# Delta attention: three groups of TensorE's queue moved behind the last key tile, two squares moved in ScalarE's

## The reference

```
q = silu(conv4(x @ Wq));  k, v = silu(conv4(x @ Wk)), silu(conv4(x @ Wv))      # 3 keys and values a token
for t:                                     # each head and batch
    S = S * exp(g_t)
    for i in range(3):
        S = S + beta_i * outer(k_i, v_i - k_i @ S)
    o_t = q_t @ S
out = (o * rsqrt(mean(o*o) + 1e-5) * rms_weight * silu(x @ Wg)) @ Wo
```

## Time and profile before

| | |
|---|---|
| time, median of 3 runs | 3211.24 us (3210.70 to 3217.59) |
| profiled execution, span | 3211.1 us |
| mean granted TensorE clock | 0.960 |
| TensorE matmul (PE) busy | 3002.0 us, 93% |
| TensorE weight load (PEld) busy | 2361.5 us, 74% |
| VectorE (DVE) busy | 2536.5 us, 79% |
| ScalarE (ACT) busy | 2251.8 us, 70% |
| GpSimd (POOL) busy | 1974.9 us, 62% |

### The profile page before, as it was taken

How to read it: one execution, slowest core, us unless ns; L and a number is a source line. 1 busy time by engine, 2 the same in 40 slices (tenths; PEclk the granted TensorE clock), 3 DMA queues, 4 the chain that set the end, 5 groups by cost and what they waited for, 6 DMA issues and landing times. The chain is left out here.

```text
span 3211.1 us, 83441 instructions
## 1 busy us (share of the span) xinstructions
PE 3002.0 (93%) x27212; PEld 2361.5 (74%) x27212; DVE 2536.5 (79%) x5859; ACT 2251.8 (70%) x6953; POOL 1974.9 (62%) x3125
## 2 busy tenths in 40 slices
PE   5569999999999999999999999999997999767999
PEld 3458888888888888888888888888876444455444
DVE  5669999999999999999999999999754454594554
ACT  4768888888888888888888888888643343412443
POOL 1588888888888888888888888888831000100000
PEclk8879999999999999999999999999998899957999
DMA  5457776767677766767777767677532332002322
GB/s 108 120 153 174 188 186 169 181 173 179 172 188 180 174 177 180 175 174 182 184 182 173 179 175 177 175 183 178 151 93 73 149 134 114 10 3 77 149 113 112
DMA packets 588205, 482.87 MB, mean 150 GB/s; under 512 B 464785, under 2 KB 504369, under 8 KB 581633
## 3 DMA queue, kind: packets, MB, share of 16 engines
q1 hardware_dynamic: 579328, 474.39, 55.8%
q10 hardware_dynamic: 8448, 3.15, 0.4%
HBM read 285.53 MB, written 191.86 MB: 149 GB/s over the span
## 5 line engine op out<-in xcount | busy, mean ns | idle before, releaser
L931 DVE SCALAR_TENSOR_TENSOR conv_k<-PP,tk,conv_k 128x256 f32<-128x256 f32 x1536 | 722.7, 479 | 61.8 <-ACT conv_k L766 33.6
L704 POOL TENSOR_TENSOR X<-X,tmp 96x31 f32<-96x31 f32 (+15 forms) x992 | 535.5, 540 | 77.7
L931 DVE SCALAR_TENSOR_TENSOR conv_v<-PP,tv,conv_v 128x256 f32<-128x256 f32 x1152 | 538.9, 477 | 44.9 <-ACT conv_v L766 35.3
L701 POOL TENSOR_TENSOR tmp<-At,X 96x31 f32<-96x31 f32 (+15 forms) x992 | 487.9, 492 | 63.1 <-DMA At<-n_d 4.9
L1100 PE MATMUL PP<-xn,wk 128*128 128x268 f32 x1024 | 341.9, 418 | 42.1 <-DVE conv_k L931 31.1
L687 POOL TENSOR_TENSOR rk<-ss,half 96x8 f32<-96x8 f32 x128 | 209.3, 1635 | 172.5 <-DVE ss L899 172.5
L669 POOL TENSOR_TENSOR Sg<-S,gend 128x512 f32<-128x512 f32 x256 | 266.8, 1042 | 60.4 <-DVE S L890 60.4
L738 ACT ACTIVATE recA<-TG,es 96x128 f32<-96x128 f32 x1024 | 285.4, 369 | 6.0 <-DVE es L924 6.0
L766 ACT ACTIVATE conv_k<-PP,tk 128x256 f32<-128x256 f32 x512 | 245.7, 482 | 58.7 <-PE PP L1100 51.9
L730 ACT ACTIVATE recA<-TG 128x128 f32<-128x128 f32 x1024 | 266.3, 273 | 24.2 <-PE TG L1151 24.2
L1064 PE MATMUL RB<-rhs,Yf 96*96 96x128 f32 x2048 | 269.0, 274 | 14.4 <-DVE rhs L879 14.4
(11 more groups left out here) (289 smaller groups left out, 6764.7 us busy)
## 6 DMA issues: line engine op xcount, KB each, us to landing
kqg_d<-kqgA SPq DMA_DIRECT2D x128, 512.0 KB, 6.1
kqgB<-kqg_d SPq DMA_DIRECT2D x128, 512.0 KB, 4.4
rec_d<-recA SPq DMA_DIRECT2D x128, 480.0 KB, 3.3
recB<-rec_d SPq DMA_DIRECT2D x128, 480.0 KB, 5.8
f1gates<-f1gates_d SPq DMA_DIRECT2D x24, 1024.0 KB, 6.6
f2gates<-f2gates_d SPq DMA_DIRECT2D x24, 1024.0 KB, 6.8
gdec<-gdec_d SPq DMA_DIRECT2D x128, 128.0 KB, 5.5
apk_d<-apkA SPq DMA_DIRECT2D x128, 128.0 KB, 3.3
```

The costliest lines, as they stand in the source:

```text
L701: nc.gpsimd.tensor_tensor(t, At[q % 2][:, j, j + 1:].unsqueeze(2).broadcast_to(sh), X[q % 2][:, j, 0:cols].unsqueeze(1).broadcast_to(sh), ...
L704: nc.gpsimd.tensor_tensor(x, x, t, ALU.subtract).then_inc(sub_ev, 1)
L931: return nc.vector.scalar_tensor_tensor(acc, src[:, :, j:j + SPAN], w[:, j:j + 1], acc, ALU.mult, ALU.add)
```

## The change

On TensorE, `wm(c)` and `o_(r, 0)` move behind `k_tile(f, 3)`, so that `wm`, both `o_` and `m3` follow one another. `o_(r, 1)` no longer waits for the square of half 0. On ScalarE both squares wait for the outputs of half 1 and stand behind `ksilu`; `w12` moves behind the first tap of the q tile, and `ksilu` ahead of the squares and `yev`. The scratch tile of the squares gets a part for each half.

```diff
-        osq = sb("osq", [128, 128])
+        osq = sb("osq", [128, NCC, 128])
...
-                need(act, o_mm[cc], N)
+                need(act, o_mm[1], N)
                 need(act, fs_ev, N - 1)
-                nc.scalar.activation(osq[:, :], o_ps[:, cc, :], ACT.Square, accum_out=mo[:, cc:cc + 1]).then_inc(mo_ev[cc], 1)
+                nc.scalar.activation(osq[:, cc, :], o_ps[:, cc, :], ACT.Square, accum_out=mo[:, cc:cc + 1]).then_inc(mo_ev[cc], 1)
...
                 tap0(f, "k1")
-                mo_(r, 0)
                 tap0(f, "k0")
                 kr(f - 1, 0)
                 vsilu(c)
                 kr(f - 1, 1)
                 tap0(f, "k2")
-                w12(c)
                 wev(r, 1)
                 q2_(f - 1)
                 tap0(f, "q")
+                w12(c)
+                ksilu(f)
+                mo_(r, 0)
                 mo_(r, 1)
                 yev(c)
-                ksilu(f)
                 qsilu(f)
...
                 need(pe, wev_ev[cc], N)
-                if cc:
-                    need(pe, mo_ev[0], N)
-                else:
+                if not cc:
                     need(pe, acc_ev, N - 1)
...
                 sr(r, 0)
                 k_tile(f, 1)
-                o_(r, 0)
                 k_tile(f, 0)
-                wm(c)
                 ks(r, 1)
                 gram(f - 1, 0)
                 k_tile(f, 2)
                 w_(r, 1)
                 gram(f - 1, 1)
                 k_tile(f, 3)
+                wm(c)
+                o_(r, 0)
                 o_(r, 1)
                 m3(c)
                 vtr(c, 1)
```

## The result

The changed kernel takes 3299.86 us (3298.34 to 3300.49, 4 runs) where the kernel before takes 3210.97 in the same session: a ratio of 1.0269, 95% interval 1.0254 to 1.0284. It is slower by 89 us; 96 were forecast. (The title counts three groups of TensorE's queue; two change their place, the merge and the output products of half 0.)

What follows compares the result with a forecast made beforehand. TensorE was taken to set the pass, with VectorE about 1.2 us to spare; 87 x 0.89 + 29 x 0.64 = 96 us, added to the median 3211.24, gave 3307 us, 8 in 10 range 3262 to 3350.

Steps and rivals of the forecast that it cites:

- TensorE's order would be stopped by k tile 0's bank: k tile 0 waits 0.33 us for VectorE's third tap of v tile 2, starting 7.98 us into the pass.
- 2.31 us from k tile 0 to `gram` 0: `gram` 0 waits for ScalarE's `kr` 0, behind the first tap of k tile 0; start at 10.29, wait 0.76 us.
- The arm over the three taps ends at the same time: VectorE's taps on k tile 0 lead to `rhs` 1, ready at 11.60, as `w_` 1 is reached at 11.70.
- The full pass 0.89 longer: `w_` 1 comes 0.65 us earlier, 1.54 of moved work follows; the full pass goes from 17.52 to 18.41 us.
- TensorE busy for about 1.2 us less: Sign expected in the profile after: TensorE's busy time about 1.2 us below a full pass of 18.2 to 18.5.
- The fourth pass 0.64 longer: In every fourth pass the 2 us copy starts 0.3 us earlier, giving back at most 0.25: 0.64 instead of 0.89.
- The edges: The last 11 passes, without a key part: taken at nothing, between -6 and +10 us in all.
- `m3` waits for nothing: ScalarE's `w12` runs within both groups of output products (0.92 us) ahead of `m3`; costed at nothing, up to 0.5 if late.
- The rival of the drains: Waits are covered and TensorE's saved drains, 0.50 us a pass, are all: 58 us faster, 3153 us; chance 0.08.
- The rival of the clock: TensorE's granted clock falls in one full pass in four after the new waits: 44 us more, 3351 us; chance 0.17.

Runs made afterwards that it cites:

- e4: The changed kernel with VectorE's `acc_` moved from ahead of the taps of v tile 2 to behind the third tap of k tile 1; 3291.89 us.
- e6: The changed kernel with ScalarE's `kr` of half 0 ahead of the first tap of k tile 0; 3437.07 us, ratio 1.0696.
- e3: The changed kernel with the output products of half 0 back ahead of k tile 0, so only the merge is moved; 3308.66 us, ratio 1.0289.
- e2: The changed kernel with the merge back behind k tile 0, so only the output products of half 0 are moved; 3246.66 us, ratio 1.0101.
- e5: The changed kernel with the merge and `w12` at their places of before and `acc_` behind the third tap of k tile 1; 3196.97 us, ratio 0.9947.
- e8: e5 with the 2 us copy of every fourth pass cut in two, the second part ahead of `wev(r, 0)`; 3173.05 us, ratio 0.9871.
- e9: e4 with GpSimd's solve cut to one column per product and difference; 3259.38 us, ratio 1.0143 to the kernel before.

## Why the prediction was right, step by step

**TensorE's order would be stopped by k tile 0's bank.** Right: 7.98 forecast, 7.97 measured, released by VectorE's conv_v. e4, which ends those taps earlier, moves k tile 0. `ks` 1 started at 8.57, 8.58 forecast.

**2.31 us from k tile 0 to `gram` 0.** Right: 10.29 forecast, 10.28 measured. The pass without a recurrence, in which this wait stands alone, gave the number. Its being a chain of two operands is what I missed: `es` had 0.19 us to spare by my count, 0.09 in the trace after, and none once the tap came earlier (e4). My 8.93 was its end in one pass, the earliest of three kinds: in the pass ahead of it, from 1200.01, it ended at 9.12. In the changed kernel it ends at 8.93, 9.02 and 9.11, and the last just binds: in the pass from 1240.98 `kr` 0 starts 0.42 behind its tap and not 0.38, and the pass takes 18.43. That is 0.05 us in one pass of four, 1.5 us in all; that it was not more was luck.

**The arm over the three taps ends at the same time.** Nearly: `rhs` 1 ended at 11.45 (11.54 forecast) and `w_` 1 started at 11.69 (11.70), so this arm had 0.18 to spare and not 0.10. Only e6 shows that it matters; forecast 3434, measured 3437.

**The full pass 0.89 longer.** 0.86 measured (18.41 and 18.38): the work behind the waits is as long as I summed it. One sign I gave was wrong: TensorE busy for about 1.2 us less. The windows show 18.38 - 17.62 = 0.76, since the profile's idle time begins at a modelled end; from start to start the waits are the 1.30 above (1.24 forecast).

**The fourth pass 0.64 longer.** Wrong in size, 0.31. I let the earlier copy give back at most the 0.25 us that TensorE waited there. But k tile 0 starts in that pass when VectorE's taps end, and these come earlier by the whole shift of the copy. In the changed kernel `At` starts at 1203.82, 0.20 ahead of its pass, and before at 1235.21, 0.16 into it, and the taps of v tile 2 end at 8.12 instead of 8.49. And k tile 0 stood 0.60 behind those taps in the fourth pass of before, against 0.42 in the full one. So it moves by 0.91, from 9.09 to 8.18 (0.60 ahead of `ks` 1, as in the full pass), where it moves by 0.37 in the full pass. This makes 29 x 0.33 = 10 us of too much, and the full passes 87 x 0.03 = 3 more. The edges, taken at nothing, brought about 3, and so 96 came out at 87 in the spans.

**`m3` waits for nothing.** Right for this change, but for a reason that I gave as a side remark: with `w12` behind the tap on the q tile, only both groups of output products between merge and `m3` cover it. With one group it costs 0.07 (e3), and with the merge early but `w12` late 0.27 (e2).

**The rival of the drains.** The time at a change of shape is real: a k tile takes 0.46 ahead of a wide product and the output products 0.44 to 0.47 ahead of each other or of `m3`, and e5 and e8, which lose two of the four changes of shape and cover the waits, have a full pass 0.16 shorter than before. By my prices of 0.09 and 0.14, less the 0.09 that k tile 0 still waits by my count (7.74 - 7.65), it is 0.14. In the changed kernel nothing of them is left, since k tile 0 and `gram` 0 start when VectorE and ScalarE allow it.

**The rival of the clock.** It did not happen: 1.00 between 225 and 2414 us, past the last full pass, with TensorE busy for 2095.3 of 2189.0 us. In the passes without a key part it still fell, in one of them (from 2493.37, 18.19 us at 0.81 instead of 15.14 at 1.00), which costs the same 3 us as the two at 0.90 before. That the waits of the earlier trace rows lowered it was no guide to the waits of the full pass. Why not, no run here shows.

## What to carry to other kernels

Work that stands between a producer and the operation waiting for it is not free to move, even on an engine that is busy all the time: before grouping operations by shape, list for every operation that moves up what releases it, on which engine, and when, and add the new wait to what the grouping saves. Here moving 1.54 us of cover to save 0.50 us of drains cost 0.86 us a pass, while moving only the 0.46 us that the rest can cover gained 0.16 in the full pass, once `w12` was left early and `acc_` made late (e5). Read such a release in every kind of pass, not in one: `es` ended at three different times. A stage at either end of a loop in which one part is missing often shows such a wait already, with its length.

## What the runs showed of the hardware that I had not expected

VectorE's `es`, 96 x 256 with both inputs in SBUF, takes 0.41 us in e9, where GpSimd's operations are short, and up to 0.92 in e4. It is not evenly slowed: it ends 0.27 to 0.29 us behind the end of the GpSimd operation that is running when it starts, or 0.41 behind its own start where that is later. This holds for every `es` between 900 and 1500 us in the kernel before, the changed one, e4 and e9, some 130 in all. So an earlier start within the same GpSimd operation gains nothing (9.02 in the changed kernel and in e4). The Trainium skill (GPSIMD Engine Reference, Specifications) says that GpSimd's SBUF interfaces are shared with VectorE, with contention for VectorE's instructions that have two inputs in SBUF. The runs agree, and put 0.32 us on this operation (735 and 411 ns median, e4 and e9). That `es` waits for the running operation is read from the times; only the length of GpSimd's operations was varied by a run.
